# Query stores on SyncE's queue, dense weights behind the second batch's own rows, key-value gathers that wait for key-value stores only

## The reference

```
mask = adj + eye
q, k, v = x@Wq.T + bq, x@Wk.T + bk, x@Wv.T + bv      # each (4096, 8, 32)
scores  = einsum('nhd,mhd->hnm', q, k) / sqrt(32);  scores = -1e9 where mask == 0
ctx     = softmax(scores) @ v                         # (4096, 256)
h1 = layernorm(x + ctx@Wo.T + bo)                     # gain and bias ln1
h2 = layernorm(h1 + relu(h1@W1.T + b1)@W2.T + b2)     # 1024 hidden features, gain and bias ln2
```

## Time and profile before

| | us |
|---|---|
| median of 3 runs | 551.79 (549.46 to 553.23) |
| profiled execution, its own time | 547.99 |
| its span | 546.2 |
| mean granted TensorE clock in it | 0.949 |
| busy: PE / DVE / POOL / ACT | 474.9 / 387.3 / 291.1 / 219.7 |

### The profile page before, as it was taken

The page is one execution under the profiler, slowest core; times in us unless marked ns, Lnnn a source line. Parts: engine busy times, 40 slices in busy tenths (PEclk is TensorE's granted clock), DMA queues, the critical chain, the costliest instruction groups (busy, mean ns, idle before and its releaser), DMA issues.

```text
span 546.2 us, 7455 instructions
## 1 busy us (share of the span) xinstructions
PE 474.9 (87%) x2306; PEld 377.6 (69%) x2306; DVE 387.3 (71%) x1066; ACT 219.7 (40%) x547; POOL 291.1 (53%) x400
## 2 busy tenths in 40 slices
PE   5999994968699899979989998989786888989993
PEld 4888883856557766865876686578445778868783
DVE  0548678548768887997999798698777378966103
ACT  1244252224352454336345334743642425353530
POOL 7545344636634566776775545426456257861202
PEclk9999998788799999999999999999898988989998
DMA  7999969898999799979979857275465757430001
GB/s 177 292 274 272 252 234 358 191 252 153 261 153 216 203 127 255 235 127 279 117 254 151 198 155 132 74 144 113 110 101 162 142 109 181 121 93 20 20 0 41
DMA packets 40058, 92.18 MB, mean 169 GB/s; under 512 B 4936, under 2 KB 17096, under 8 KB 39888
## 3 DMA queue, kind: packets, MB, share of 16 engines
q0 software_dynamic: 17792, 59.80, 54.8%
q1 hardware_dynamic: 20432, 30.02, 15.8%
q10 hardware_dynamic: 1792, 1.85, 1.0%
HBM read 123.61 MB, written 16.80 MB: 257 GB/s over the span
## 4 chain that ended last, share of the span: by engine, by line
PE 54%; DVE 16%; issue 8%; ACT 8%; DMA 6%; POOL 6%; POOLq 0%; ACTq 0%; DVEq 0%
PE ps L1110 18%; PE ps L1123 11%; PE ps L1825 10%; DMA q_table<-slots 4%; PE ps L869 3%; ACT xT_all L1174 2%; PE ps L1100 2%; DVE stats L1184 2%; PE ps L872 2%; POOL slots L1035 2%; DMA work<-q_table,row_of 1%; POOL rstd L1226 1%; PE ps L1090 1%; PE ps L1841 1%; DMA early<-in_wqkvT 1%
## 5 line engine op out<-in xcount | busy, mean ns | idle before, releaser
L1110 PE MATMUL ps<-xT_all,w 128*128 128x512 f32 (+1 forms) x320 | 123.2, 533 | 3.1 <-ACT xT_all L1164 2.9
L1123 PE MATMUL ps<-w,xT_all 128*128 128x256 f32 x512 | 121.5, 392 | 3.1 <-ACT xT_all L1164 3.1
L1123 PEld LDWEIGHTS ps<-w,xT_all 128*128 128x128 f32 x512 | 98.2, 197 | 16.8 <-ACT xT_all L1164 3.8
L1110 PEld LDWEIGHTS ps<-xT_all,w 128*128 128x128 f32 x320 | 61.2, 201 | 45.3 <-issue 34.9
L1035 POOL DMA_INDIRECT slots<-kv_table,col_of x54 | 55.0, 1019 | 50.1 <-DVE col_of L613 38.5
L1027 POOL DMA_INDIRECT slots<-kv_table,found x48 | 51.8, 1079 | 44.8 <-PE ps L872 22.0
L1164 ACT ACTIVATE xT_all<-ps,col_table 128x512 f32<-128x512 f32 (+1 forms) x80 | 47.8, 603 | 61.3 <-PE ps L1110 61.3
L1825 PE MATMUL ps<-early,xT_all 128*128 128x256 f32 x256 | 59.6, 395 | 6.2 <-DMA early<-in_wqkvT 6.2
L1825 PEld LDWEIGHTS ps<-early,xT_all 128*128 128x128 f32 x256 | 50.4, 199 | 14.0 <-DMA xT_all<-in_xT 4.6
L525 DVE MAX8 adj_bytes<-adj_bytes 128x8 f32<-128x1024 f32 (+5 forms) x40 | 38.2, 973 | 19.0 <-DMA adj_bytes<-in_adj 19.0
L1042 POOL DMA_INDIRECT work<-q_table,row_of x40 | 44.5, 1114 | 11.2 <-issue 11.2
(11 more groups left out here) (177 smaller groups left out, 877.2 us busy)
## 6 DMA issues: line engine op xcount, KB each, us to landing
adj_bytes<-in_adj POOLq DMA_DIRECT2D x31, 512.0 KB, 11.3
kv_table<-slots POOLq DMA_DIRECT2D x7, 1024.0 KB, 14.2
xT_all<-in_xT SPq DMA_DIRECT2D x13, 512.0 KB, 19.2
slots<-kv_table SPq DMA_DIRECT2D x12, 512.0 KB, 9.7
q_table<-slots POOLq DMA_DIRECT2D x16, 256.0 KB, 8.2
q_own<-q_table SPq DMA_DIRECT2D x12, 256.0 KB, 11.1
out_dram<-early SPq DMA_DIRECT2D x6, 512.0 KB, 3.6
slots<-in_adj SPq DMA_DIRECT2D x1, 2048.0 KB, 24.3
```

What stands on the lines that cost most here:

```text
L1110: last = nc.tensor.matmul(ps[:, q["bank"] + f % 2, 0:q["g"] * P], w1[:, k, f * P:(f + 1) * P], q["h1T"][:, k, :], start=(k == 0), stop=(k ...
L1123: nc.tensor.matmul(to, q["ffT"][:, f, j * P:(j + 1) * P], w2[:, f, :], start=(f == 0), stop=False)
```

## The change

Three things move; all arithmetic stays as it is.

1. `store_q` moves from POOL's program to SP's. Pair 0 is stored ahead of step 0's own rows, pairs 1 to 5 behind them, pairs 6 to 11 in SP's step 0 and pairs 12 to 15 in its step 1, each behind `load_own` of the next step.
2. The five weight loads move from behind step 0's own rows to behind step 1's own rows (SP's step 0).
3. `tables_ready` is split: `kv_ready` for the key-value stores and `queries_ready` for the query stores. `gather_aligned` and `gather_edges` call the first alone (but for tile 0's batch), `gather_queries` and the second load of `load_own` call the second.

```diff
-        def tables_ready(eng, q):
+        def kv_ready(eng):
             for i in range(STAGES):
                 eng.wait_ge(s_kv_out[i], (GROUPS // STAGES if i < STAGES - 1 else GROUPS // STAGES - 1) * 16)
-                if q.first:
-
+            eng.wait_ge(s_kv_last, 2 * 16)
+
+        def queries_ready(eng, q):
+            if q.first:
+                for i in range(STAGES):
                     eng.wait_ge(s_q_out[i], PAIRS // STAGES * 16)
-
-            eng.wait_ge(s_kv_last, 2 * 16)
             pair = (q.no + q.T - 1) // 2
             eng.wait_ge(s_q_out[pair % STAGES], (pair // STAGES + 1) * 16)
...
         def gather_edges(pool, q, us=None):
             pool.wait_ge(cols_ready, q.p + 1)
-            tables_ready(pool, q)
+            kv_ready(pool)
+            if q.first:
+                queries_ready(pool, q)
...
         def gather_queries(pool, q):
             pool.wait_ge(row_ready, q.b + 1)
+            queries_ready(pool, q)
...
         def load_own(sp, q):
-            tables_ready(sp, q)
+            kv_ready(sp)
...
+            queries_ready(sp, q)
             sp.dma_start(q_own[q.par][:, 0:q.T, :], q_tiles[q.no // 2][:, q.no % 2:q.no % 2 + q.T, :]).then_inc(own_loaded[q.par], 16)
...
+            def store_q(i):
+                sp.wait_ge(s_q, i + 1)
+                sp.dma_start(q_tiles[i], q_stage[i % STAGES].rearrange("p (t d) -> p t d", d=D)).then_inc(s_q_out[i % STAGES], 16)
+
+            store_q(0)
             load_own(sp, STEPS[0])
-            for dst, src in ((wo, woT.rearrange("(k p) n -> p k n", p=P)), (w1, w1T.rearrange("(k p) n -> p k n", p=P)),
...
+            for i in range(1, Q_BEFORE):
+                store_q(i)
             for q in STEPS:
                 i = q.b
                 n, place, count = step_of_job(q)
                 if i + 1 < NB:
                     load_own(sp, STEPS[i + 1])
+                if i == 0:
+                    for dst, src in ((wo, woT.rearrange("(k p) n -> p k n", p=P)), (w1, w1T.rearrange("(k p) n -> p k n", p=P)),
...
+                for gap in range(6):
+                    for p in q_pairs(i, gap):
+                        store_q(p)
                 if i == 2:
                     load_own(sp, TILE0)
                 if place == 1 and q.group <= WIDE_JOBS:
...
-            store_q(0)
             gather_aligned(pool, STEPS[0])
             gather_edges(pool, STEPS[0])
             gather_queries(pool, STEPS[0])
-            for i in range(1, Q_BEFORE):
-                store_q(i)
...
-                for p in q_pairs(i, 0):
-                    store_q(p)
...
-                for p in q_pairs(i, 2):
-                    store_q(p)
-                for gap in range(3, 5):
-                    for p in q_pairs(i, gap):
-                        store_q(p)
```

More of the change, by code:

```diff
@@ L1479, in _ @@
                     load_own(sp, STEPS[i + 1])
+                if i == 0:
+                    for dst, src in ((wo, woT.rearrange("(k p) n -> p k n", p=P)), (w1, w1T.rearrange("(k p) n -> p k n", p=P)),
+                                     (w2, w2T.rearrange("(k p) n -> p k n", p=P))):
+                        sp.dma_start(dst[:], src).then_inc(s_weights, 16)
+                    for name, src in (("g2", g2), ("be2", be2)):
+                        sp.dma_start(rows[name][:], src.to_broadcast([P, D])).then_inc(s_weights, 16)
+                for gap in range(6):
+                    for p in q_pairs(i, gap):
+                        store_q(p)
                 if i == 2:
@@ L1550, in _ @@
             pool.dma_start(kv_dram[1 + N:, :], zero_rows[1:]).then_inc(s_pad, 16)
-            def store_q(i):
-                pool.wait_ge(s_q, i + 1)
-                pool.dma_start(q_tiles[i], q_stage[i % STAGES].rearrange("p (t d) -> p t d", d=D)).then_inc(s_q_out[i % STAGES], 16)
             pool.wait_ge(s_bias, 16)
```

## The result

The changed kernel takes 559.22 us (median of 4 runs, 559.12 to 560.77), the kernel before 552.06 on the same chip (4 runs, 549.46 to 553.23). The ratio is 1.0162, with a 95% interval of 1.0128 to 1.0197: **slower by 7.2 us** between the medians, where 7.4 were forecast. The two medians alone give 1.0130, at the low end of the interval; the ratio is worked out over all the runs, and 1.62% of 552 us would be 8.9 us. So the cost is known to lie between some 7 and 11 us. The profiled execution of the changed kernel took 559.26 us, with a span of 557.4.

What follows compares the result with a forecast made beforehand. PE was taken to bound most of the span, a relay of engines the stretch before attention at 135.33. Attention 6.7 us later, gains counted in, plus 0.7 for the clock gave +7.4: 551.8 to 559, range 549.5 to 565.

Steps and rivals of the forecast that it cites:

- Part 1: The head, before DVE's first edge scores: gathers wait for key-value stores alone, which gains at most 1.1 us.
- Part 2: Stall before 119.6: pair 7's store in time, pair 8's landing at 117.2; net gain 2.6 us, the head's gain included.
- Part 3: Job 0's x load, now behind pair 15's store, lands at 140.6; attention starts at 142.0, not 135.33: +6.7 us.
- The clock: Job 0's attention: PE, after idling some 10 us, runs more groups at its lower clock level, +0.7 us.
- The rest: From attention's start to the end: the same length as before, some 411 us.
- The rule weighed: DMA engines alternate between queues by packet: one store slips through between the adjacency loads, pair 7 in time: 559.
- SP's transfers get their share: Rival, SP's transfers beside adjacency loads: stall gain 7.2 us, attention at 133 to 137, say 551.5; chance 0.27.
- part 2 gives nothing: Rival: pair 7's store is caught at the adjacency pair's start or behind the weights, +10 to +13 us, 563; chance 0.17.
- The faster case: Rival, PE at steps 0 and 2: shorter waits keep the 2.4 GHz level, -6.2 us, 545.6; chance 0.05.

Runs made afterwards that it cites:

- before: The kernel before, unchanged, in its first profile: the profiled execution took 547.99 us.
- before_again: The kernel before, unchanged, profiled once more: 550.32 us.
- x_late: The kernel before with only job 0's x load held back until all query pairs are copied: 562.44 us, ratio 1.0237.
- split_only: The kernel before with only the wait split, key-value gathers no longer behind query stores: 548.43 us, ratio 0.9949.
- x_ahead: The changed kernel with job 0's x load issued behind step 2's own rows, ahead of the stores of pairs 12 to 15: 547.41 us, ratio 0.995.
- adj_after_x: The changed kernel with step 1's adjacency pair issued only after job 0's x columns have landed: 554.09 us, ratio 1.005.
- slots8: The changed kernel with eight staging slots for query pairs instead of four: 557.8 us, ratio 1.0144.
- slots8_x_early: The changed kernel with eight staging slots and job 0's x load in SP's step 0 right behind the weights: 544.93 us, ratio 0.9912.
- x_early_4: The changed kernel, still with four staging slots, with job 0's x load in SP's step 0 right behind the weights: 548.44 us, ratio 0.9957.
- weights_back: The changed kernel with the five weight loads back behind step 0's own rows, ahead of the stores of pairs 1 to 5: 560.82 us, ratio 1.0181.
- after_again: The changed kernel, unaltered, profiled once more: 560.73 us.
- after: The changed kernel in its first profile: the profiled execution took 559.26 us.

## Why the prediction was right

**Part 1, -1.1.** The idle time ahead of DVE's first edge scores is gone in all nine profiles with the split wait, so the direction and the cover (DVE's own searches) were right. The size is less certain than the 1.6 us of one pair of profiles (89.61 against 91.18): the nine start at 89.39 to 91.46, 90.2 in the mean, and the three with the old wait at 91.05 to 91.90, 91.4 in the mean. That is 1.2 us.

**Part 2, pair 7 in time, pair 8 at 117.2.** Pair 7's store was issued at 99.6, 1.2 us ahead of the pair, and landed in 3.3 us; pair 8's at 101.73, 0.9 behind the pair's first issue, and took 16.2 us, to 117.9. The copies came at 109.40 (forecast 111) and 118.03 (117 to 118). The copy of pair 15 was done at 129.9, forecast 130.7: so parts 1 and 2 gained 3.4 us there, not 2.6. Part 2 alone can be read from the time between DVE's first edge scores and the copy of pair 15, which leaves part 1 out: 41.6, 42.4 and 41.8 us in `before`, `before_again` and `x_late`, 41.8 in `split_only`; 39.7, 39.3, 39.8 and 39.6 in the two profiles of the change, `x_ahead` and `adj_after_x`. So part 2 brings 2.3 us, where the forecast had 1.5 (2.6 less 1.1). In the time it is not seen: `x_ahead`, which has both parts, gains 0.5%, and `split_only`, which has part 1 alone, the same; the two intervals leave room for up to 1.8 us between them.

**Part 3, attention at 142.0.** x issued at 130.29 (forecast 131.3), landed at 140.5 (140.6), attention at 141.99 (142.0). Each of the three causes was put to the test: the issue behind pair 15 (`x_ahead`, `x_late`), the adjacency pair in front (`adj_after_x`), and ACT's order, by which the bias waits at once (`slots8`: a sooner copy only lengthens that wait). The near equality is partly luck: x was issued 1.0 us sooner than forecast and landed 3.5 us behind the second adjacency load, which itself was 0.9 later than forecast; the 4.5 us that I had taken for it was too much (3.3 us in `slots8`, 2.0 in `x_late`).

**The clock, +0.7.** From attention to the lists it took 5.38 us (141.99 to 147.37) against 4.99: +0.4. Only the first two groups were slow (2.05 and 1.81 us of timeline); the third took 1.03. But that pair of profiles makes it look small, since the first profile of the kernel before was partly slow there itself. A later landmark is DVE's aggregation of job 0's first statistics (L1190 of the kernel before), here in `x_late` and in `slots8_x_early`:
```profile
156.23 0.38 DVE L1190 BATCH_NORM_AGGREGATE mv<-stats 128x2 f32<-128x6 f32 x4
```
```profile
134.62 0.38 DVE L1196 BATCH_NORM_AGGREGATE mv<-stats 128x2 f32<-128x6 f32 x4
```
It comes 9.5 us behind attention in the first and 6.6 in the second. In the five profiles in which x was in time and the first attention matmuls took 1.09 or 1.10 us (`before_again`, `x_ahead`, `x_early_4`, `slots8_x_early`, `split_only`) it is 6.6 us, in the first profile of `before` 8.3, and in the six in which attention waited for x (`adj_after_x` the least) 8.1 to 9.6, 8.9 in the mean. So a late x costs some 2 us more behind attention than a kernel in time has to pay. The term was too small for that, and the low figure of the first profile hid it.

**The rest, same length.** The medians differ by 7.2 us, against 7.4, and that near equality is luck too: the first profile of the kernel before, from which the sum was made, is an execution 4 us shorter than its median, that of the changed kernel is at its median, and the two pairs of profiles differ by 11.3 and by 10.4 us. In the first pair of profiled executions the same length does not hold: 411 us from attention to the end before, 415.4 after. Up to 232 us the changed kernel is 6.9 us behind the kernel before; it loses 3.3 us more between there and 326, and the last 1.0 after the last computation (DVE's last piece in the chain starts at 540.88 before and at 551.01 after, the spans end at 546.2 and 557.4). The windows view, the same work in the kernel before and in the changed one:
```profile
226.00:246.00 20.00, 17.19 (x99) 14.42 (x98) 19.28 (x56) 6.39 (x15) 14.27 (x18) 1.00 0.84 206
```
```profile
232.90:252.90 20.00, 17.20 (x95) 14.81 (x94) 18.72 (x54) 5.64 (x14) 13.45 (x18) 0.91 0.83 203
```
PE is busy for the same 17.2 us with a granted clock of 0.91 and not 1.00, and gets through fewer instructions. Over the twelve profiles of this study the stretch from attention to the end took 410.9 to 416.8 us, whatever was changed ahead of it; in the six where attention waited for x it took 414.5 in the mean, where it was in time about 412.6. The difference is that of the first ten microseconds (the clock, above). From the first aggregation to the last one at that line, in `x_late` and in `slots8_x_early`
```profile
544.35 0.25 DVE L1190 BATCH_NORM_AGGREGATE mv<-stats 128x2 f32<-128x6 f32 x2
```
```profile
522.60 0.25 DVE L1196 BATCH_NORM_AGGREGATE mv<-stats 128x2 f32<-128x6 f32 x2
```
it is 388.1 and 388.0 us, though attention starts 18.7 us apart. The shortest, 387.6, are those of `before` and `weights_back`, one early and one late; `after_again` has 388.1, `before_again` 390.2, `x_early_4` 390.5, `after` and `slots8` 390.7, `x_ahead` 391.5, `split_only` 392.2, `adj_after_x` 392.5. So the long stretch has no order by how late x was: "same length" was right up to a scatter of 5 us. Why single executions differ by that much is open.

**The rule weighed.** The Trainium skill, "DMA: Bandwidth & Descriptors", section "Queues, rings and completion order", has each DMA engine take turns between queues, a whole packet at a time. The sum by it was 559, with pair 7 in time, and that came out. But the reason I gave, that one store would slip through between the first and the second adjacency load, was not tested by pair 7, which was through before the pair began to matter (3.3 us). It was tested by pair 8, alone inside the pair, and there it failed: the first load landed at 112.2, the second at 117.6, and the store at 117.9. **The time was right by this step; its reason was not.** The rows taken strictly (an SP transfer inside a pair lands behind its second load) described pair 8 better, and pair 7 was just outside them.

**The rivals.** Their chances add up to 0.46 for "same" and 0.05 for "faster", 0.01 off what is said under Numbers. That SP's transfers get their share is refuted by the 16.2 us of pair 8's store and the 10.2 of x. That part 2 gives nothing because pair 7's store is caught is refuted by pair 11's copy at 109.40; that its 2.3 us reach the end is not shown. The faster case, attention early enough to keep the 2.4 GHz level, needed x within 5 us of its issue; it did not happen in the change, and it is what `slots8_x_early` made: the first four attention matmuls in 1.10 us, and 5.0 us less than before (by the medians).

## What to carry to other kernels

When stores are moved to another engine's queue, list what that queue has behind them: a store that waits for the last result of a phase holds back every load after it, and a load that was hidden with 11 us to spare becomes the longest piece of the chain. Loads that wait for nothing new go ahead of stores that wait for a computation; here that one move was worth 2% of the time. And before a stall is removed, look at what bounds the next meeting point of the engines: with x late, 5.3 us taken off the stall brought 1.4 us at attention. Each part is worth a run of its own, too: the split wait alone gave the same 0.5% as the whole change with its load put right.

## What the runs showed of the hardware

- A 256 KB store issued 1.2 us before a pair of adjacency loads landed in 3.3 us; one issued 0.9 us after the first of the pair's issues took 16.2 us, 0.3 us past the second load. Other profiles have the same two stores: 4.2 us (1.2 ahead) and 15.7 (1.0 after) in `after_again`, 3.9 (0.6 ahead) and 13.1 (2.4 after) in `x_ahead`. The view of the store's issue line, for the one at 99.6 and the one at 101.7:
```profile
DMA to landing us min/median/max: 3.3/3.3/3.3
...
DMA to landing us min/median/max: 16.2/16.2/16.2
```
- It is not absolute: in `x_ahead` the x load, issued at 115.47 with about 2 us of one pair left and 6.6 us before the next pair's issue, took 11.0 us, and had landed at 126.5, 4.4 us into the next pair. A transfer that is well under way when a pair starts is not held until its end. What sets the border between the two was not measured.
- Kernels whose work is the same from attention on differ by up to 4.6 us in that stretch (410.9 to 415.5; 416.8 in `adj_after_x`, which has some of its loads in it), and the mean granted clock of the span goes from 0.934 to 0.954 over the profiles. The time of one kernel scatters as much: `x_ahead` gave 544.61 to 549.93 us in ten runs.
